# The turned product U2 D3 moves to the end of a pair of tiles, and ScalarE takes the rank copies before two splits

## The reference, cut to what matters

```
x = x + x W^T + 2 * sum_e gate_e(x) * B_e (A_e x)      # L0: 8 experts, two chosen by softmax, rank 16
x = x + weights[condition] mixed over the 64 rows      # L1: a 64 x 64 matrix for each batch entry
x = x + A2[id] (B2[id] x)                              # L2: an adapter of rank 16 for each batch entry
x = x + x W3^T + b3 + 2 * (x A3[id]) B3[id]            # L3: rank 16 for each batch entry, and a bias
```

## Time and profile before

| | |
|---|---|
| median of 3 runs (lowest to highest) | 909.32 us (906.81 to 909.46) |
| profiled execution: its time, its span | 909.15 us, 907.4 us |
| PE busy | 894.5 us (99%) |
| DVE busy | 584.5 us (64%) |
| ACT busy | 346.0 us (38%) |
| POOL busy | 237.9 us (26%) |
| mean granted TensorE clock | 0.998 |

### The profile page before, as it was taken

The page is one execution under the profiler, slowest core; times in us unless marked ns, Lnnn a source line. Parts: engine busy times, 40 slices in busy tenths (PEclk is TensorE's granted clock), DMA queues, the critical chain, the costliest instruction groups (busy, mean ns, idle before and its releaser), DMA issues.

```text
span 907.4 us, 14951 instructions
## 1 busy us (share of the span) xinstructions
PE 894.5 (99%) x4726; PEld 791.7 (87%) x4726; DVE 584.5 (64%) x1575; ACT 346.0 (38%) x800; POOL 237.9 (26%) x379
## 2 busy tenths in 40 slices
PE   9999999999999999999999998999999999999997
PEld 7888888888888889899999997998998989989987
DVE  6554454454367427668678666787686687686786
ACT  5544333333334333343433433424424334334333
POOL 2010110010010013532522523415416325235240
PEclk9999999999999999999999999999999999999999
DMA  6988786999663564656665765666666567667665
GB/s 241 310 263 281 215 256 208 304 344 247 198 196 122 172 199 135 201 167 190 214 187 177 219 189 155 199 205 195 186 192 216 173 177 219 190 180 217 184 195 157
DMA packets 105604, 187.71 MB, mean 207 GB/s; under 512 B 15926, under 2 KB 66870, under 8 KB 105526
## 3 DMA queue, kind: packets, MB, share of 16 engines
q1 hardware_dynamic: 105526, 186.76, 67.1%
HBM read 143.20 MB, written 49.81 MB: 213 GB/s over the span
## 4 chain that ended last, share of the span: by engine, by line
PE 81%; DVE 5%; SPq 4%; DMA 4%; POOL 3%; issue 3%; ACT 1%; DVEq 0%; POOLq 0%
PE ps_o L1406 27%; PE ps_d L1432 14%; PE ps_w L1440 11%; PE ps_s L1406 9%; PE ps_d L1440 7%; PE ps_o L1453 4%; PE ps_d L1447 4%; DMA mdraw<-t 2%; PE ps_o L1464 2%; SPq L446 2%; PE ps_s L1470 1%; POOL stat_raw L719 1%; DMA stat_raw<-x 1%; POOL rows_raw L719 1%; PE ps_w L1447 1%
## 5 line engine op out<-in xcount | busy, mean ns | idle before, releaser
L1043 DVE TENSOR_TENSOR stat_lo<-stat_raw,stat_hi 128x1024 fp32r<-128x1024 f32 (+1 forms) x127 | 144.0, 1134 | 30.2 <-ACT stat_hi L774 27.9
L774 ACT ACTIVATE stat_hi<-stat_raw 128x1024 fp32r<-128x1024 f32 (+1 forms) x127 | 116.8, 933 | 23.5 <-POOL stat_raw L658 8.4
L1432 PE MATMUL ps_d<-w_hi,stat_hi 128*128 128x512 f32 x256 | 103.9, 406 | 0.0
L1432 PE MATMUL ps_d<-w_lo,stat_hi 128*128 128x512 f32 x256 | 101.8, 398 | 0.0
L1432 PE MATMUL ps_d<-w_hi,stat_lo 128*128 128x512 f32 x256 | 101.7, 397 | 0.0
L1406 PE MATMUL ps_o<-chunk_a_hi,stat_hi 128*128 128x512 f32 x216 | 84.4, 391 | 0.5 <-DVE stat_lo L1043 0.4
L1406 PE MATMUL ps_o<-chunk_a_hi,stat_lo 128*128 128x512 f32 x216 | 84.1, 389 | 0.0
L1406 PE MATMUL ps_o<-chunk_a_lo,stat_hi 128*128 128x512 f32 x216 | 84.0, 389 | 0.0
L683 POOL CAST w_hi<-mdraw 128x512 fp32r<-128x512 f32 x32 | 19.7, 615 | 211.0 <-DMA mdraw<-t 211.0
L658 POOL TENSOR_TENSOR stat_raw<-stat_raw,ident 128x128 f32<-128x128 f32 x40 | 23.1, 579 | 183.5 <-DMA stat_raw<-stat 183.5
L1406 PE MATMUL ps_o<-chunk_b_hi,stat_hi 128*128 128x512 f32 x152 | 59.1, 389 | 0.0
(11 more groups left out here) (223 smaller groups left out, 2285.7 us busy)
## 6 DMA issues: line engine op xcount, KB each, us to landing
up<-tu SPq DMA_DIRECT2D x124, 256.0 KB, 4.1
stat_raw<-stat SPq DMA_DIRECT2D x59, 512.0 KB, 4.3
mdraw<-t SPq DMA_DIRECT2D x128, 208.0 KB, 3.0
stat_raw<-x SPq DMA_DIRECT2D x32, 512.0 KB, 3.5
out<-outb SPq DMA_DIRECT2D x30, 512.0 KB, 5.4
t<-md_a SPq DMA_DIRECT2D x16, 576.0 KB, 6.0
rows_raw<-x SPq DMA_DIRECT2D x32, 256.0 KB, 3.7
chunk_a_raw<-mov SPq DMA_DIRECT2D x24, 256.0 KB, 5.6
```

The source lines that it names most:

```text
L774: return nc.scalar.activation(dst, src, ACT.Copy)
L1043: return nc.vector.tensor_tensor(out=dst, in0=src, in1=rounded.bitcast(F32), op=ALU.subtract)
L1432: last = nc.tensor.matmul(plain_bank(t)[:, 0:WCOLS], rows[a][:, k, :], w[c][:, k, :], start=k == 0 and m == 0, stop=k == KB - 1 and m == l ...
```

## The change

`vsum` becomes two buffers, by the tile's parity. DVE no longer turns U2 D3 of tile a in `fore` nor that of b behind `La_raw`: both go to the end of the step, a's in front of `plain_lo(b)` and b's in front of `mix_lo(a)`. In the last pair a's comes behind `fore`, b's in front of `plain_lo(b)`, and `La_lo` goes behind `mix_lo(TURN_B)`. ACT takes `after_P1`, `h2T_copy(a1)` and `h3_hi(a1)` before `ud_hi(b)` and `mix_hi(b1)`. No instruction is added or dropped.

```diff
-        vsum = sb("vsum", [BR, BR])
+        vsum = [sb(f"vsum{n}", [BR, BR]) for n in range(2)]
...
                 gate_exp(a)
+                after_P1(j)
+                if back:
+                    h2T_copy(a1)
+                    h3_hi(a1)
                 ud_hi(b)
-                after_P1(j)
-                if back:
-                    h2T_copy(a1)
+                if back:
                     mix_hi(b1)
-                    h3_hi(a1)
                     h3T_copy(a1)
...
                 s_lo(j, 0)
-                hidden_rows(a)
                 if back:
                     h3_lo(a1)
...
                 La_raw(j)
-                hidden_rows(b)
                 hgT_lo(b)
                 La_lo(j)
                 if back:
                     h2_lo(b1)
                 Rb_raw(j)
+                hidden_rows(a)
                 plain_lo(b)
                 Rb_lo(j)
+                hidden_rows(b)
                 mix_lo(a)
...
             def last(j):
                 fore(j, True, True)
+                hidden_rows(a)
                 add_bias(a1)
...
                 hgT_lo(b)
-                La_lo(j)
+                hidden_rows(b)
                 plain_lo(b)
                 mix_lo(TURN_B)
-                hidden_rows(b)
+                La_lo(j)
                 h3_lo(b1)
```

More of the change, by code:

```diff
@@ L978, in fore @@
                 gate_exp(a)
-                ud_hi(b)
                 after_P1(j)
@@ L982, in fore @@
                     h2T_copy(a1)
+                    h3_hi(a1)
+                ud_hi(b)
+                if back:
                     mix_hi(b1)
-                    h3_hi(a1)
                     h3T_copy(a1)
@@ L1229, in hidden_sum @@
                 dve.wait_ge(dve_vparts, 2 * t + 2)
-                nc.vector.tensor_tensor(out=vsum[:, :], in0=vhi[:, :], in1=vlo[:, :], op=ALU.add).then_inc(dve_vsum, 1)
+                nc.vector.tensor_tensor(out=vsum[t % 2][:, :], in0=vhi[:, :], in1=vlo[:, :], op=ALU.add).then_inc(dve_vsum, 1)
             def hidden_rows(t):
-                both = vsum[:, :, None].to_broadcast([BR, BR, 2])
+                both = vsum[t % 2][:, :, None].to_broadcast([BR, BR, 2])
                 dve.wait_ge(dve_vsum, t + 1)
```

## The result

The changed kernel takes 899.43 us, median of seven runs (898.13 to 903.85), against 906.81 (904.75 to 909.46) for the one before: ratio 0.9919, 95% interval 0.9896 to 0.9941, so 7.4 us less. The forecast was 903.5, with 899.5 to 907.5 as its range: the time is 4.1 better than forecast and just outside.

What follows compares the result with a forecast made beforehand. PE was taken as the bound, with only its standing and clock losses to win. From the profiled 909.15 us, 5.5 + 1.15 + 0.3 + 0.75 = 7.7 removed and 2.1 added at the tail gave 903.5, range 899.5 to 907.5.

Steps and rivals of the forecast that it cites:

- What bounds it: PE is busy 894.5 of 907.4 us; only its 13 us of standing and its clock's losses can be won.
- The front pairs, 5.5: PE's waits at `h3_rows(a1)` and small ones at `ranks2` in thirteen pairs go: 5.5 us removed.
- Had either alone been moved, the other would have kept part: At `h3_rows(a1)`, DVE's `hidden_rows(a)` and ACT's late `h3_hi(a1)` both delay PE; moving one leaves part of the stall.
- The tail, 2.1: At the tile's end, the second turn delays `mix_lo(a)` into POOL's S sums, stalling PE's `h3_rows(b2)`: 2.1 us added.
- six near pairs: Pairs where `mix_lo` started 0.15 after to 0.36 before POOL's S sum; colliding costs 0 to 0.8 each, 1.5 in sum.
- Rival 1: The tail costs nothing, as DVE gets its turns between POOL's instructions: 901.4 us, 898 without a late load; chance 0.22.
- double miss: Second turn's last cast falls behind the first S sum, `mix_lo` behind the second; `h3_lo(b2)` 1.29 us or more later.
- The late load, 0.75: With `mdraw` late, PE stops at `plain(b)` instead of `ranks2(a1)`: 0.75 us won, 2.1 of standing stay, clock taken at 0.
- Before and behind the pairs, 1.15 and 0.3: Same waits before the pairs, 1.15 us removed; in the last pair `Rb_raw` no longer behind `hidden_rows(b)`, 0.3 removed.
- 2: Rival: every pair collides at the tail, 14 x 0.4 = 5.6 us added against 7.7 removed: 907.0 us; chance 0.14.
- 4: Rival: `h3_hi(a1)` in its new place waits on something hidden, the stall only changes its name: 907 us; chance 0.06.
- 3: Rival: at the tail the second turn misses two places in six near pairs, 9.9 us added: 911 us; chance 0.08.

Runs made afterwards that it cites:

- the turns alone: Only DVE's two turns moved, ACT's order as before, in the kernel before: 903.93 us against 905.49, ratio 0.9979.
- ACT's order alone: Only ACT's new order of copies, turns where they were, in the kernel before: 902.03 us, ratio 0.9966; measured again 902.04 us, ratio 0.9936.
- the second trace of the changed kernel: The changed kernel measured again with nothing altered, against the kernel before: 900.82 us, ratio 0.9929.
- the kernel with `h3_hi` alone in front: The kernel before with one exchange on ACT, `h3_hi(a1)` ahead of `mix_hi(b1)`: 905.47 us, ratio 0.998.
- the changed kernel with late loads: The changed kernel with SP reading a tile's ids twice before loading `mdraw`, so these loads come late in all 14 pairs: 928.21 us, ratio 1.0232.
- the two kernels with late loads made regular: SP reads a tile's ids twice before loading `mdraw`: on the kernel before 943.93 us, ratio 1.0399; on the changed kernel 928.21 us, ratio 1.0232.
- the one with two idle turns: The changed kernel with eight extra DVE transposes between `hidden_rows(b)` and `mix_lo(a)`: 919.04 us (only two runs), ratio 1.0125.

## Why the prediction was wrong in size, by its own steps

*What bounds it.* Right: what was won is PE's standing and, in the profiled runs, its clock.

*The front pairs, 5.5.* Held: the 13 pairs without the late load went from 453.05 to 447.70, 5.35 less, with the tail's part in it. "Had either alone been moved, the other would have kept part" is right for the turns alone (4.8 left) and wrong for ACT's order alone (1.4 left, in the second pair, and nothing in these 14). The sum was right, its attribution incomplete: the move of `ud_hi(b)` was costed at nothing and has a gain, through POOL. POOL's two subtractions take 2.4 in their new place (1.22 and 1.19 from 623.34 on), not 1.5, and still no wait of PE comes of it.

*The tail, 2.1: the step that failed.* I took `mix_lo(a)` as 0.3 to 0.6 later in every pair and let six near pairs collide, 2.1 in sum; measured is 0.2, no more than before. The waiting was as estimated, 0.55 in one cast in 12 of the 14 pairs, but I put all of it on `mix_lo`: the turn without any wait takes 1.53, not 1.6, and the gap has room for some 0.4 of it, so `mix_lo` comes about 0.16 later. And a near margin does not make a collision. Of my six, `mix_lo` had gone first in four, by 0.02 to 0.37, and lost nothing; in two of these the sum took 1.39 and 1.42 instead of 1.29. In the changed kernel it goes first in 13 pairs, as at 747.93. Only one of the 14 met the sum, with its last cast, and PE lost 0.20. DVE in that pair:

```profile
403.60 1.23 DVE L1247 CAST udb<-vturned 128x32 fp32r<-128x32 f32 x1
404.74 0.28 DVE L1044 TENSOR_TENSOR mix_lo<-mix_raw,mix_hi 128x128 fp32r<-128x128 f32 x1
```

POOL there:

```profile
403.49 1.29 POOL L719 TENSOR_TENSOR stat_raw<-stat_raw 128x512 f32<-128x512 f32 x1
```

The sum of the waits stands at 0.2, as before. Rival 1 describes it. That this trace holds no worse pair is partly luck: the second trace of the changed kernel has a double miss.

The Trainium skill, "SBUF — State Buffer", section on two separate sides, has the pair of ports as an exclusive lock between GpSimd and an instruction of DVE that is in a two-port mode or has two inputs in SBUF (the latter only while GpSimd reads SBUF): whichever starts first holds it for the whole instruction, the other fully blocks. `mix_lo` at 613.09, with two inputs, agrees, and so does the cast at 436.02, if it runs in such a mode, which no row shows. The four transposes at 437.04 have one input and run with POOL's sum beside them from 437.07, unstretched; none of the 128 transposes of the turns in this trace is stretched (199 to 206 ns each). So of a turn of seven instructions only three are seen to be open to the lock, and only 0.6 us of its length. I had priced the turn's waits from these three, and the rest of the error is the gap's room.

*The late load, 0.75.* Mis-sized: this pair gave back 3.55, from 38.99 to 35.44. PE in it:

```profile
761.16 0.47 PE L1434 MATMUL ps_d<-w_hi,stat_hi 128*128 128x512 f32 x1 [0.80 <-issue]
```

The place of the wait is as predicted, and POOL's cast of `w_lo` ended at 760.45 + 0.61 = 761.06. The rest is this: that cast was late for PE by 0.7, where in the run before it was late by 1.7 (557.68 against 557.92 - 2.61 + 0.65 = 555.96, where `plain(b)` would have been due; so 1.8 of standing would have stayed there, with the 0.10 to the start, not 2.1); and PE's busy time in the pair fell from 36.38 to 34.64, as the clock stayed at 1.00. 0.75 + 1.0 + 1.74 = 3.49. The first is the change's, the second chance; of the third I had said that no row tells, and took 0. After 2.61 us of standing the clock went to 0.96 over the pair, after 0.80 it stayed. That is no rule: in the kernel with `h3_hi` alone in front a stand of 2.44 was followed by 1.00, and in the changed kernel with late loads one of 2.98 by 1.00 and one of 2.84 by 0.96. PE after the first of these, and the stretch behind it:

```profile
558.57 0.43 PE L1497 MATMUL ps_o<-up,h2T 128*128 128x344 f32 x1 [2.44 <-ACT h2T L774]
...
559.00:594.00 35.00, 34.80 (x204) 32.08 (x204) 24.33 (x77) 13.35 (x38) 13.94 (x22) 1.00 0.61 180
```

Without the two kernels with late loads made regular and the one with two idle turns, the traces hold twelve late loads: the seven late loads with ACT's `h2T_copy` in front cost PE 0.85 to 1.04 each, the five with it behind `ud_hi(b)` 0.9 to 2.8. It follows that the profiled run of before was a poor base: its 909.15 holds a late load that cost 4.6, and the median of seven is 906.81, not the 909.32 of the first three. "The profiled one is typical" was wrong.

*Before and behind the pairs, 1.15 and 0.3.* 0.73 and 0. The start's own waits differ by some 0.4 between the two executions. At the end S3's product comes 0.27 behind the transpose in front of it (882.20 against 881.93), before 0.36: `Rb_raw` moved, but then waited 0.47 for PE's own product before it, and by the end of the span nothing is left of the 0.1.

The balance against 903.5: tail 2.1 better, late load 2.8 better, start 0.4, end 0.3 and front 0.15 worse; 4.05, and the profiled run is 4.0 below. Against medians, in which the one late load of the profiled runs weighs less, 7.4 was won, and 5.5 + 1.15 + 0.75 = 7.4 had been priced, with neither end nor tail: the tail, 2.1 too dear, and the end, 0.3 too much, are then what was wrong. That the two agree to 0.1 is luck, as the interval of the ratio leaves room from 5 to 9 us.

*The rivals.* 2 and 4 fell; 3 was seen once. What the turns themselves add to ACT's order is 1.2 us (902.04 against 900.82); the second pair's 1.4 alone would be as much. The two ranges overlap, so the size is not sharp.

*Left open:* why single loads of `mdraw` land late, and why the profile calls PE's wait for `w_lo` "issue".

## What to carry to other kernels

Order an engine's copies by when their inputs are ready and when the bottleneck wants the result; one copy in front that waits for a third engine holds up all behind it (3.83 us at 697.06, of which PE paid nearly 1), and the label on the bottleneck can then name the wrong engine. When a piece of work moves, ask not only who waits for it but whom it used to disturb: here POOL's two subtractions stretched a chain on DVE that the trace showed as slow but did not blame on them. Price a delay against its cover as a margin from start to start in each pair, after taking off what the idle time in front of it absorbs, and take the base from a median of several runs where the profiled one holds a rare event.

## What the runs showed of the hardware that was not expected

- Transposes of 32 x 32 on DVE, from SBUF to SBUF, are not stretched beside POOL's work, and POOL's is not beside them (0.85 for four and 0.46, at 437.04 and 437.07); casts and subtractions of DVE at the same place are (0.18 to 1.23, 0.29 to 1.42).
- POOL pays too. Its subtractions of U2 and D3 take 0.75 and 0.74 at 626.96 and 627.66, where DVE's gates were stretched, and 1.22 at 623.34, beside DVE's splits. An S sum that started 0.01 behind `mix_lo` took 1.43 instead of 1.29.
- A stand of PE of 2.61 us was followed by a pair at 0.96 of the full clock, but stands of 2.44 and 2.98 by pairs at 1.00.
